# Attention with a talking-heads mix on one core: the mix as 64x64 blocks of a pair, and another deal of TensorE's work over the turns

## What is computed

```python
q = l2norm(x @ Wq), k = l2norm(x @ Wk)             # 16 heads of 64; 4 memory keys in front of k
dots = einsum('bhid,bhjd->bhij', q, k) * QK_SCALE
dots = einsum('hg,bgij->bhij', W_pre_th, dots)     # the mix ahead of the softmax, over the heads
dots = where(causal, mask_value, dots)             # token i sees keys j <= i and the 4 memories
vk   = top_k(dots, 64)[0][..., -1:]                # only the 64 largest of a row are kept
attn = softmax(where(dots < vk, mask_value, dots))
attn = einsum('hg,bgij->bhij', W_post_th, attn)    # the mix behind the softmax
out  = einsum('bhij,bhjd->bhid', attn, v)
return (out * head_scale * sigmoid(x @ Wg + bg)) @ Wo
```

## Times and profile before

| | us |
|---|---|
| median of 3 runs (2402.21 to 2410.45) | 2406.95 |
| the profiled execution | 2402.8 |
| its span, first to last instruction | 2401.0 |

### The profile page before, as it was taken

One profiled execution on the slowest core, in us unless ns is written; L12 is line 12 of the kernel. 1 busy time (PEld: TensorE's weight loads), 2 busy tenths in 40 slices (PEclk: granted clock), 3 DMA queues, 4 the chain that ended last, 5 costly groups with the idle time before them and its releaser, 6 DMA issues. The chain is left out here.

```text
span 2401.0 us, 55203 instructions
## 1 busy us (share of the span) xinstructions
PE 2104.1 (88%) x16059; PEld 1363.1 (57%) x16060; DVE 1801.4 (75%) x7282; ACT 1622.8 (68%) x4700; POOL 812.5 (34%) x2274
## 2 busy tenths in 40 slices
PE   7995789898999998899989988998898889884997
PEld 3433456665566556665666666666666666563433
DVE  6564489868986898689868986898689868983446
ACT  4442578757876787678767885888588758871543
POOL 3001444344434433443344334433443344311000
PEclk9996899999999999999999999999999999997998
DMA  5002012101210121012101210121012101212001
GB/s 171 0 9 75 22 38 60 42 25 42 59 42 25 42 60 42 25 42 60 42 25 42 60 42 25 42 59 42 25 42 60 42 23 40 57 37 85 0 1 70
DMA packets 113218, 104.71 MB, mean 44 GB/s; under 512 B 34448, under 2 KB 110864, under 8 KB 112912
## 3 DMA queue, kind: packets, MB, share of 16 engines
q1 hardware_dynamic: 108000, 96.65, 15.8%
q10 hardware_dynamic: 4912, 4.46, 0.6%
HBM read 19.14 MB, written 12.71 MB: 13 GB/s over the span
## 5 line engine op out<-in xcount | busy, mean ns | idle before, releaser
L1491 DVE TENSOR_SCALAR_CACHE_REDUCE S<-S,minus_thr 128x68 f32<-128x68 f32 (+56 forms) x456 | 218.0, 514 | 225.6 <-POOL minus_thr L1388 224.8
L1048 PE MATMUL bankC<-R,E 128*128 128x128 f32 x2560 | 349.9, 286 | 34.6 <-POOL R L1395 34.6
L1048 PEld LDWEIGHTS bankC<-R,E 128*128 128x128 f32 x2560 | 337.3, 201 | 70.7 <-POOL R L1395 36.7
L1032 PE MATMUL bankB<-raw,mixpre 128*128 128x76 f32 (+37 forms) x1024 | 357.8, 437 | 19.3 <-DMA raw<-SC 19.2
L1244 ACT ACTIVATE S<-bankB,aim_first 128x68 f32<-128x68 f32 (+56 forms) x456 | 231.2, 510 | 201.5 <-PE bankB L1032 199.7
L1379 POOL TENSOR_TENSOR S<-S,diagmask 128x8 f32<-128x8 f32 x512 | 108.6, 216 | 688.2 <-ACT S L1244 654.7
L1022 PE MATMUL bankD<-KT,QT 64*64 64x258 f32 (+7 forms) x2304 | 195.6, 409 | 94.2 <-ACT SC L1233 86.0
L1395 POOL TENSOR_SCALAR R<-mixpost,rinv 128x128 f32<-128x128 f32 x512 | 184.8, 374 | 180.1 <-DVE rinv L1555 179.7
L1551 DVE SCALAR_TENSOR_TENSOR E<-S,limit,E 128x68 f32<-128x68 f32 (+56 forms) x456 | 221.2, 521 | 30.4 <-DVE E L1551 0.3
L1270 ACT ACTIVATE E<-S,nmax 128x12 f32<-128x12 f32 (+56 forms) x512 | 233.2, 505 | 14.5 <-POOL nmax L1409 14.5
L1074 PEld LDWEIGHTS bankM<-PT,V 128*64 128x64 f32 x5120 | 183.9, 141 | 102.4 <-issue 85.9
(11 more groups left out here) (176 smaller groups left out, 3968.8 us busy)
## 6 DMA issues: line engine op xcount, KB each, us to landing
X_first<-in_L_attn_x_dram ACTq DMA_DIRECT2D x8, 512.0 KB, 9.6
x<-X_first SPq DMA_DIRECT2D x8, 512.0 KB, 2.9
xt<-x SPq DMA_DIRECT2D x32, 128.0 KB, 2.4
x<-xt SPq DMA_DIRECT2D x32, 128.0 KB, 2.5
X_last<-x SPq DMA_DIRECT2D x8, 512.0 KB, 6.6
out_dram<-X_last SPq DMA_DIRECT2D x8, 512.0 KB, 2.8
raw<-SC SPq DMA_DIRECT2D x8, 258.0 KB, 3.0
raw<-SC SPq DMA_DIRECT2D x8, 254.0 KB, 3.5
```

The costliest lines, as they stand in the source:

```text
L1032: last = nc.tensor.matmul(bankB[n % 2][:, 0:wide(n)], W.mixpre[:, :], raw[n % RAWS][:, 0:wide(n)], start=True, stop=True)
L1048: last = nc.tensor.matmul(bankC[n % 2][:, jb * P:(jb + 1) * P], E[n % EBUFS][:, jb * P:(jb + 1) * P], R[n % RBUFS][:, :], start=True, stop ...
L1491: nc.vector.tensor_scalar(row, row, minus_thr[:, col(n)], None, ALU.add, ALU.max, accum_out=rmax[:, col(n)]).then_inc(max_done, 1)
```

## The change

1. **The mix.** `mixpre` is now 64 columns wide and each group is laid out in `raw` as two parts of 4 tokens, 64 rows (4 tokens by 16 heads) each; the two groups of a pair lie in the lower and the upper 64 partitions of one `raw` buffer. `mix_pair` makes four matmuls of 64x64 blocks for a pair, two groups by two parts, where there were two of 128x128. The layout inside `QT` (`qT`) and of the mix matrices (`own4`, the loads of the constants) follows.
2. **Raw buffers.** RAWS is 4, each for a pair, so that all of a half lies in them. SP issues two DMAs for a group where it was one. SBUFS is 6 where it was 8: `evict` of a pair now waits for `select_pair` of the pair three turns back.
3. **Both mixes and both evictions stand at the start of the turn**, where other work lay between them. `mix_pair` waits until both evictions of the pair before are done.
4. **The deal of PE's work.** Quarter 3 of the second half's scores goes from the head of turn 6 to the tail of turn 4. The next tile's first quarters go from turns 10, 12, 12, 14 to turns 10, 10, 12, 12 (heads and tails). The gates go from turn 6, both halves, to the tails of turns 10 and 12, one half each (in the first tile turns 12 and 14). `project` goes from turn 8 to 6. The first tile's v goes from turn 4 to 2. DVE's `ln_stats` goes from turn 2 to 0.

```diff
-SBUFS = 8
+SBUFS = 6
-PROJECT_AT = 8
-GATES_AT = (6, 6, 6, 6)
-V0_AT = 4
+PROJECT_AT = 6
+GATES_AT = (12, 10, 10, 10)
+V0_AT = 2
-RAWS = 6
+RAWS = 4
+QUARTER = IG // 2
...
             for n in range(NG):
                 u, g = divmod(n, IG)
                 wait_read(sp, score_all(u)[-1])
-                if n >= RAWS:
-                    sp.wait_ge(mixed, n - RAWS + 1)
+                pair, r = divmod(n, 2)
+                if pair >= RAWS:
+                    sp.wait_ge(mixed, pair - RAWS + 1)
                 w = group_width(n)
-                sp.dma_start(raw[n % RAWS][:, 0:w], SC[g:P:IG, :, 0:w]).then_inc(raw_in[n % RAWS], 16)
+                for part in range(2):
+                    sp.dma_start(raw[pair % RAWS][HALF * r:HALF * r + HALF, part, 0:w],
+                                 SC[2 * g + part:P:2 * IG, :, 0:w]).then_inc(raw_in[pair % RAWS], 16)
...
-            def mix(n):
-                pe.wait_ge(raw_in[n % RAWS], 16 * (n // RAWS + 1))
-                if n >= 2:
-                    pe.wait_ge(S_out, n - 1)
-                last = nc.tensor.matmul(bankB[n % 2][:, 0:wide(n)], W.mixpre[:, :], raw[n % RAWS][:, 0:wide(n)],
-                                        start=True, stop=True)
...
+            def mix_pair(n0):
+                pair = n0 // 2
+                pe.wait_ge(raw_in[pair % RAWS], 64 * (pair // RAWS + 1))
+                if n0:
+                    pe.wait_ge(S_out, n0)
...
+                for part in range(2):
+                    cols = slice(HALF * part, HALF * part + HALF)
+                    for r in range(2):
+                        rows, w = slice(HALF * r, HALF * r + HALF), wide(n0 + r)
+                        last = nc.tensor.matmul(bankB[r][cols, 0:w], W.mixpre[rows, :], raw[pair % RAWS][rows, part, 0:w],
+                                                start=True, stop=True, skip_group_check=True)
                 last.then_inc(mixed, 1)
...
                 if live:
-                    mix(n0)
+                    mix_pair(n0)
...
-                    if g == 6:
-                        score(2 * t + 1, 3)
                     if g == 8 and ahead:
                         turn_qk(t + 1, 0, "qT")
+                    if g == 10 and ahead:
+                        score(2 * t + 2, 0)
                     if g == 12 and ahead:
-                        score(2 * t + 2, 1)
-                    if g == 14 and ahead:
-                        score(2 * t + 2, 3)
-                    mix(n0 + 1)
+                        score(2 * t + 2, 2)
...
+                    if g == 4:
+                        score(2 * t + 1, 3)
                     if g == 4 and ahead:
                         tokens(t + 1, "k", Wk)
                     if g == 8 and ahead:
                         turn_qk(t + 1, 1, "kT")
                     if g == 10 and ahead:
-                        score(2 * t + 2, 0)
+                        score(2 * t + 2, 1)
                     if g == 12 and ahead:
-                        score(2 * t + 2, 2)
-                    if g == gates_turn(t):
-                        gates(t)
+                        score(2 * t + 2, 3)
+                    if g - gates_turn(t) in (0, 2):
+                        gates(t, (g - gates_turn(t)) // 2)
...
             def evict(n):
-                act.wait_ge(mixed, n + 1)
+                act.wait_ge(mixed, n // 2 + 1)
                 if n >= SBUFS:
                     act.wait_ge(E_ready, n - SBUFS + 1)
```

More of the change, by code:

```diff
@@ L736, in attention_phase @@
         SC = sb("SC", [P, IG, J])
-        raw = [sb(f"raw{i}", [P, J]) for i in range(RAWS)]
+        raw = [sb(f"raw{i}", [P, 2, J]) for i in range(RAWS)]
         S = [sb(f"S{i}", [P, J]) for i in range(SBUFS)]
@@ L985, in tokens, with gates, emit @@
                     pe_use(pe, (what, j, half), emit)
-            def gates(j):
+            def gates(j, half):
                 x = xnT[j % 2]
-                for half in range(2):
-                    def emit():
-                        for q in range(4):
-                            for k in range(2):
-                                lo = (4 * half + q) * P
-                                last = nc.tensor.matmul(bankD[:, half, q * P:(q + 1) * P], Wg[:, k, lo:lo + P],
-                                                        x[:, k, MEM:MEM + P], start=k == 0, stop=k == 1)
-                        return last
-                    pe_use(pe, ("g", j, half), emit)
+                def emit():
+                    for q in range(4):
+                        for k in range(2):
+                            lo = (4 * half + q) * P
+                            last = nc.tensor.matmul(bankD[:, half, q * P:(q + 1) * P], Wg[:, k, lo:lo + P],
+                                                    x[:, k, MEM:MEM + P], start=k == 0, stop=k == 1)
+                    return last
+                pe_use(pe, ("g", j, half), emit)
             def turn_qk(j, i, what):
@@ L1199, in memory_values, with gates, emit @@
                                   a["mem_v"].rearrange("h m d -> m h d")).then_inc(mem_in, 16)
-            def gates(j):
-                if j >= GBUFS:
+            def gates(j, half):
+                if j >= GBUFS and half == 0:
                     act.wait_ge(projected, j - GBUFS + 1)
-                for half in range(2):
-                    def emit():
-                        for q in range(4):
-                            pair = 4 * half + q
-                            last = nc.scalar.activation(gate[j % GBUFS][:, pair, :], bankD[:, half, q * P:(q + 1) * P],
-                                                        ACT.Tanh, bias=W.bgh[:, pair:pair + 1], scale=0.5)
-                        return last
-                    act_use(act, ("g", j, half), emit)
+                def emit():
+                    for q in range(4):
+                        pair = 4 * half + q
+                        last = nc.scalar.activation(gate[j % GBUFS][:, pair, :], bankD[:, half, q * P:(q + 1) * P],
+                                                    ACT.Tanh, bias=W.bgh[:, pair:pair + 1], scale=0.5)
+                    return last
+                act_use(act, ("g", j, half), emit)
             def qT(j):
@@ L1227, in score @@
                 if q == 0 and u:
-                    for n in range(IG * u - RAWS, IG * u):
-                        act.wait_ge(raw_in[n % RAWS], 16 * (n // RAWS + 1))
+                    for pair in range(IG // 2 * u - RAWS, IG // 2 * u):
+                        act.wait_ge(raw_in[pair % RAWS], 64 * (pair // RAWS + 1))
                 for s in score_steps(u, q):
@@ L1307, in _ @@
                         values(t, "v")
-                    if g == 6:
-                        score(2 * t + 1, 3)
                     if g == 8 and ahead:
                         qT(t + 1)
+                    if g == 10 and ahead:
+                        score(2 * t + 2, 0)
                     if g == 12 and ahead:
-                        score(2 * t + 2, 1)
-                    if g == 14 and ahead:
-                        score(2 * t + 2, 3)
-                    evict(n0 + 1)
+                        score(2 * t + 2, 2)
                 for n in ranked_in(n0):
@@ L1583, in _ @@
                     row_max(n0 + 3)
-                if g == 2 and t + 2 < NT:
+                if g == 0 and t + 2 < NT:
                     ln_stats(t + 2)
```

56 lines of the change are left out of this document (31 added, 25 removed).

## The result

The changed kernel takes **2624.64 us** (median, 2623.22 to 2626.44), the kernel before 2406.84 us beside it: a ratio of 1.091, with an interval of 1.089 to 1.093. It is slower by 218 us, 9%. The forecast was 2471 us with a range to 2535. The sign is right; the loss is 3.4 times what was forecast, and outside the range. One run further down (`e8_deal_only`, 2699.2 us beside 2645.6) was in the slower of two states of the chip, and no comparison uses it.

A forecast was written before the change was run, and what follows sets the result against it. PE sets the pace in narrow tiles; PE, ACT and DVE form a ring in wide ones. Savings and new waits nearly cancel (+1 us a sequence), slow clock adds 8.4; seven sequences at +9.3 give 2471 us, range 2360 to 2535.

The forecast's parts named there:

- the size of the waits: Gates and k, behind scores in the tail, wait for ACT to copy the bank; 3.4 us in the third tile's turn 10.
- The line through two points: Scaled tail waits with tile width from 2.27 us at 164 columns and 3.4 us at 356.
- the clock's term: Seven long waits a sequence each bring a slow stretch at 1.2 us: 8.4 us, bounds 0 and 12.
- the saving of the mix: Mixes in 64x64 blocks save PE 0.2 to 0.85 us a pair by tile, 17 us a sequence.
- the wait for `R` at the seam of two sequences: First tile, turns 0 to 8: this wait and slow matmuls behind it go, 4.1 us off.
- the cost of changing between block sizes: The drain at a change of tiling mode on PE is already inside a score set's 0.92 us.
- Edits at nothing: Ring of 6 `S`, two raw DMAs a group, earlier `project` and `ln_stats`, loads and constants: no cost.
- Hidden waits: Rival: DVE sets the pace in the wide tiles and hides PE's waits; 2290 us, chance 0.20.
- Clock stays up: Rival: no new slow stretches follow PE's waits; 2405 to 2410 us, no change, chance 0.09.
- Short ring: Rival: DVE late at the seam or fourth tile holds ACT's evictions; 2500 to 2530 us, chance 0.09.
- No overlap: Rival: the mix's 64x64 blocks don't run side by side, so it costs as before; 2607 us, chance 0.04.

The follow-up runs named there:

- e8_deal_only: The kernel before with only the new deal of PE's work, keeping its own mix, ring of 8 S and raw buffers: 2645.6 us, one run.
- e4_attend_first: The changed kernel with PE's `attend` moved ahead of the tail's scores, projections and gates: 2483.81 us, ratio 1.034.
- e9_fill_more: The changed kernel with useless matmuls on PE in the tail's waits, as many as each wait holds: 2532.12 us, ratio 1.054.
- c1_best: The order of `c2_best_old_mix` with the mix in blocks, its raw tiles, two DMAs a group and the ring of 6: 2411.94 us, ratio 1.003.
- c2_best_old_mix: The kernel before with scores two groups sooner, first tile's v in turn 2, and tails ordered projections, `attend`, scores: 2378.76 us, ratio 0.990.
- e6_before_sbufs6: The kernel before with a ring of 6 S in place of 8: 2424.5 us, ratio 1.009.

## Why the prediction was right and wrong

**Right: the mechanism and the size of the waits.** The gates in turn 10 of the third tile waited 3.01 us (forecast 3.4), those of the second tile 2.4 and 2.5 (2.7 and 2.8), of the fourth 3.2 and 3.8 (4.1 and 4.1), of the first 1.65 (1.9), means over six sequences. k waited 0.8, 2.2 and 2.7 (0.3, 2.3, 3.1), and in the fourth tile 3.6, split over two places (4.7). The line through two points was a few tenths high. The waits of the gates and of k have 198.4 us together (over 150 forecast), turns 0 to 8 are shorter in every tile and turns 10 to 14 longer, and DVE idles longer. `e8_deal_only` and `e4_attend_first` show that this is the cause.

**The step that failed: the size of the clock's term, and the saving of the mix that it was set against.** A sequence was to take 9.3 us more and takes 30.4. The prediction let seven slow stretches follow the seven longest waits, at 1.2 us each: 8.4 us, with 12 as the bound. It had this price from the one stretch of the earlier trace rows, where a short `attend` stood behind the wait. Three things were off. There were more stretches: in the trace's record of the clock the fourth sequence has eleven at 0.50, of 3.4 to 10.2 us, six in the third and fourth tile and five in the first two, where none was counted. They were longer: 62 us in all, 5.6 us each. And what stood in them was dearer: half of the gates, all dense matmuls, lost 1.7 us by itself (3.78 against 2.05). Nor does the length of the wait decide it alone: in the second tile the gates took 2.05 us behind a wait of 2.43, and 3.53 us behind one of 2.50.

The old slow stretches had been taken off the sum, so the 8.4 us stand against up to 31, half of the 62. That is an upper bound, as not every slow matmul lies on the path. At the rate of `e9_fill_more`, a third of a microsecond for each at 0.50, they cost some 21 us (an estimate), 12 more than forecast and over half of the miss. What is shown is 92 us for the clock in the whole run, by `e9_fill_more`, which still had stretches at 0.50 left. The Trainium skill, "TensorE: Matmul & The Clock Gate", Part 1, has the ramp at under 1% of a typical span; the prediction set its bound above that rule, and the measurement, up to 31 of 269.7 us, lies far above both.

`e8_deal_only` cuts the miss the other way. The forecast's own sum for it, without the 17 us of the mix, is 26 us a sequence, and it measured 30.3. So with the old mix the terms are short by 4 us; the other 17 of the miss are the whole saving of the mix, which the sequences of the changed kernel don't show. The two ways agree in the clock: `e8_deal_only` has 32 us of the sequence at 0.50 (0.94 over 269.65), the changed kernel 62. At the rate above, the 30 us more at half clock are some 10 of the 17 (an estimate), and some 7 were never there, as the part on the mix below shows. That the slow clock took what the blocks did save is the likely reading; it was not tested.

**A saving that didn't come.** In the first tile 4.1 us were taken off for the wait for `R` at the seam of two sequences. In its place stands a new one, of PE for ACT's copy `PT`, and Wq behind it takes 4.90 us:

```profile
1038.89 3.75 PE L1062 MATMUL bankC<-R,E 128*128 128x128 f32 x16 [3.10 <-ACT PT L1293]
1042.44 4.90 PE L989 MATMUL bankD<-Wq,xnT 128*128 128x512 f32 x8
```

ACT is still at work on the widest pair of the fourth tile when PE reaches the first turn. It was in the kernel before, too, where its copy ended 0.4 us ahead of the `turn` that the wait for `R` held until 954.77:

```profile
953.33 1.05 ACT L1280 COPY PT<-bankC 128x512 f32<-128x512 f32 x2
```

The wait for `R` had covered this one, and taking it off the sum took off a wait that was there twice. The 3.10 us and the 1.2 us that Wq takes beyond 3.67 are half of the 8.5 us by which the first window (44.0 for 35.5) was missed.

**The mix: busy time right, worth wrong.** PE's group fell to 190.5 us, further than the 220 expected. The prediction took the cost of changing between block sizes to be inside the 0.92 us of a set. A part of it lies behind the set: from the end of what stands before it to its own end, `turn` with 12 instructions took 1.33 us before (1103.30 to 1104.63) and 1.34 in turn 8 above, behind 128x128 matmuls (1187.55 to 1188.89), but 1.53 in turn 10, behind 64x64 blocks (1194.10 to 1195.63). 0.2 us go each time that `turn` comes right behind such blocks; before, a 128x128 mix always stood between.

How much the blocks save can be read from the changed kernel and `e8_deal_only`, whose turns have the same work on PE but for the mix: 21 of the 32 turns of a sequence stand at full clock in both traces at least once. With the waits taken off, turn 10 of the third tile takes 8.04 us for 8.66, as forecast, but turn 14, without scores in its head, takes 5.78 for 6.17: 0.39 us saved and not 0.65. The mean of the 21 is 0.32 us a pair, some 10 us a sequence (an estimate) and not 17. At a fixed order `c1_best` is 33 us slower than `c2_best_old_mix`; with the two DMAs at 54, the ring at 21 and the pair at the start at 4, the blocks themselves are worth some 46 us, 6 a sequence. This is an estimate: it takes the parts as additive, which wasn't tested, and the ring's price from the old order.

**Edits at nothing.** Two had a price: the ring, 21 us, and the two DMAs, 54. For the ring the prediction read from turn 10 of the third tile that DVE is past the point, and that at the seam PE waits anyway. At the seam it is ACT that waits, for DVE (19.7 us in `e6_before_sbufs6`), and PE's later work behind it. "SP has a turn more of time for them" is true only together with the earlier scores, and of what hides them nothing was priced as gone. Neither explains the result, since `e8_deal_only` has neither and is slower still.

**The rivals.** Hidden waits (2290): false, DVE's idle time rose by 123 us. Clock stays up (2405 to 2410): false. Short ring (2500 to 2530): real in the kernel before, but far smaller than the loss. No overlap (2607): nearest in time and false in its reason, as the mix fell to 190.5 us; it came near because the saving did not come through. The range had no case for a slow clock that costs more than 12 us a sequence, nor for a saving in PE's work that the clock takes back.

**What stays open.** Of the 126 us that `e9_fill_more` still loses, the split between waits and the slow stretches left was not measured. That the clock took back the saving of the mix is argued from the mean clocks alone, and `e8_deal_only`, on which it rests, is one run; the filling matmuls were not tried on it.

## What to carry to other kernels

In an engine that works in order, put what waits for another engine behind everything that is ready: the same operations with `attend` ahead of the waiting gates were 141 us faster. Price a new wait with the dense matmuls behind it at half clock (here 5.6 us of them on average, and up to 10.2), and look at the waits of 1.65 to 2.5 us too. A buffer's depth or a second DMA is free only as long as the cover that hides it stays; take one part at a time onto the old order before calling it free.

## What was not expected of the hardware

A wait of 3.01 us went with 10.2 us at a granted clock of 0.50, and with several waits close together it was there for half of the time (0.75 over 34.30 us), and for 7 of 17.63 us where the waits were 1.65 and 1.99 us (0.80). TensorE working on useless matmuls through the waits gained 92 us. With the new deal, mixes that took less of TensorE's time left a sequence as long as it was (269.67 and 269.65 us), at a lower granted clock (0.89 and 0.94). Twelve instructions of 128x128 took 0.2 us longer right behind 64x64 blocks than behind 128x128 matmuls (1.53 and 1.34 us). And SP spent a median of 0.59 us on issuing a DMA of 64 rows, and 0.55 us on one of 128.
